# Routing steps of four links over half-batches a partition, and the light layer's first product behind them

## The chip, the cores and the metric

One core of a Trainium2 chip runs the whole kernel. The metric is the device time of one execution in microseconds; lower is better.

## What is computed

A decoder layer on x [2, 2048, 512]: self-attention with relative-position bias, cross-attention to 77 context tokens, and a feed-forward part with two layers, each block as x + f(layernorm(x)). The feed-forward part is what matters here: a light layer for every token, and a heavy one for the 512 tokens per batch that a coordinate descent of 50 steps picks.

```python
def ffn(x, gamma, w1, b1, w2, b2):
    h = rms_norm(x, gamma)
    h = jax.nn.gelu(h @ w1 + b1, approximate=False)
    return h @ w2 + b2
s = jnp.einsum('bnd,d->bn', x, routing_token)
constant = EPS * jnp.log(K_ROUTE)             # EPS 0.1, K_ROUTE 8
b0 = -jax.nn.relu(s)
def step(carry, _):                           # 50 times
    a_prev, b = carry
    a = constant - EPS * jax.nn.logsumexp((s + b) / EPS, axis=-1, keepdims=True)
    b = -jax.nn.relu(s + a)
    return ((a, b), None)
scores = jnp.exp((s + a + b) / EPS)
sel_scores, sel_idx = jax.lax.top_k(scores, 512)
light_out = ffn(x, light weights, hidden 256)       # all tokens
routed_out = ffn(x[sel_idx], heavy weights, hidden 2048)
```

## The kernel before

The program has three parts, each with its own order of instructions on every engine: `attention` (its last product of probs and v starts at 3013.6 us), `middle` (from 3072.4 us), which leaves the layer-normed tokens in DRAM, transposed and split in two terms (`scr["t3"]`), the tokens with what is to be added (`scr["xb"]`) and the routing values s (`scr["s"]`), and `routed` (from 3694.56 us), which the change touches. Nothing is scheduled by a tool: each engine (PE, ScalarE, VectorE, GpSimd, and SP, which issues the DMAs) has a list written out by hand, and semaphores tie the lists together.

In `routed` the values of both batches lie as `s_max` [128, 2, 16], token 128 t + p in partition p, with the maximum of a batch in a 17th column. A step (L1783 to L1797) takes on VectorE the minimum of s and the negated level (`low`) and the difference to its last column (`dif`), on ScalarE the Exp (L1713), on PE a product with a matrix of ones, which adds the 128 partitions and leaves 32 sums in every partition (L1609), on VectorE the sum of each batch's 16 (`total`, L1794), on ScalarE the Ln (L1715), on VectorE the new level (`neg_a`, L1797). PE then has work of its own between two steps: from the third step on, four matmuls of the light layer's first product (`hidden_of`, L1593), 192 in all, in eight chunks of 512 tokens with 24 matmuls each (two halves of the hidden size x 12 terms), so that they end with the last step. VectorE copies each finished half-chunk out of PSUM (`hidden_out`, L1772). ScalarE splits the light weights at step 0 (`wl1_hi`, L1719, which waits for the load of w1l), VectorE makes the rest of them at step 1 (`wl1_lo`, L1789), and from step 33 on ScalarE scales one of 16 pieces of the heavy layer's w1 behind each step (L1727).

SP loads the values, w1l and its gamma, chunks 0 and 1 of the tokens (`tokens_in`, L1522: two parts of 1 MB each into a buffer of two chunks), the light layer's w2, then chunk ch as soon as chunk ch - 2 has been multiplied, with four tiles of xb behind chunk 2 and the heavy layer's w1, the small constants and the rows b2 and places behind chunk 3.

Behind the steps come the scores (L1800 to L1807), 64 matmuls that spread them over the partitions (L1617), their copy (`rows`, L1731), the gelus of the light layer on ScalarE (L1736), five levels of a search for the 512th score (first L1830) with the light layer's second product between them, the choice and gather of the tokens, and the heavy layer (L1682 to L1704). VectorE waits for all weights ahead of `gain` (L1814), which comes before the first level.

## Time and profile before

| what | value |
|---|---|
| timed runs | 4121.46, 4125.23, 4127.27 us; median 4125.23 |
| profiled execution | 4132.32 us, its span 4130.5 us |
| granted TensorE clock, mean over the span | 0.974 |
| PE busy | 3930.1 us (95%), 18711 matmuls |
| VectorE / ScalarE / GpSimd busy | 58% / 49% / 65% |
| DMA | 350.50 MB, mean 85 GB/s |

All times inside the execution are counted from the start of the span. PE is busy nearly throughout, but this is an average over parts that differ; which engine or wait ends last in the stretch that is changed has to be read from that stretch. A matmul's busy time overlaps with that of the next, so the distance from start to start tells the rate.

### The profile page before, as it was taken

Reading aid. Unit: us, or ns where it says so; the run is one execution under the profiler, and the core shown is the slowest. Engines: PE = TensorE matmul, PEld = TensorE weight load, DVE = VectorE, ACT = ScalarE, POOL = GpSimd, SP = SyncE. Lnnn points to the kernel's source line nnn. Section 1 sums busy time; section 2 is a strip of 40 time slices with the busy share of each in tenths; the row PEclk is TensorE's granted clock in tenths of the full one; section 3 lists DMA queues with packets and bytes.
Section 4 is the critical chain, followed back from the end, with each engine's and each line's share of the span. In section 5 each row is a group of like instructions: output and inputs, shape, how many; then the busy total and the mean of one; then the engine's idle time right before and its main releaser. Section 6 shows DMA issues by size and latency. Waiting matters only on the chain. (4 is left out here: it accounts for less than half of the span.)

```text
span 4130.5 us, 59273 instructions
## 1 busy us (share of the span) xinstructions
PE 3930.1 (95%) x18711; PEld 2160.6 (52%) x18711; DVE 2411.3 (58%) x3315; ACT 2014.5 (49%) x3385; POOL 2693.8 (65%) x1406
## 2 busy tenths in 40 slices
PE   7979999999999999999999999999959999967899
PEld 6754444444444444444444444444338888854344
DVE  3346666666666666666666666666316777754400
ACT  2225555555555555555555555555424555533010
POOL 1008888888888888888888888888933444410010
PEclk9979999999999999999999999999979999979999
DMA  6632222232223342232222322232032333335610
GB/s 187 168 90 73 67 62 56 75 88 61 57 59 94 87 122 56 59 99 62 61 56 82 82 61 56 59 96 63 14 113 75 108 102 105 101 105 186 207 31 10
DMA packets 393921, 350.50 MB, mean 85 GB/s; under 512 B 193131, under 2 KB 267371, under 8 KB 392808
## 3 DMA queue, kind: packets, MB, share of 16 engines
q1 hardware_dynamic: 325864, 326.29, 27.2%
q10 hardware_dynamic: 66048, 16.78, 1.8%
q0 software_dynamic: 1920, 6.29, 0.5%
q8 instruction: 49, 0.80, 0.1%
q14 instruction: 40, 0.33, 0.0%
HBM read 142.89 MB, written 89.70 MB: 56 GB/s over the span
## 5 line engine op out<-in xcount | busy, mean ns | idle before, releaser
L254 POOL TENSOR_TENSOR acc<-acc,probs 128x1024 f32<-128x1024 f32 x896 | 2131.7, 2379 | 266.1 <-ACT probs L664 139.7
L771 DVE TENSOR_REDUCE maxes<-ps 128x1 f32<-128x1024 f32 x1024 | 1250.7, 1222 | 672.5 <-PE ps L482 667.9
L667 ACT ACTIVATE probs<-ps,far_bias 128x1024 f32<-128x1024 f32 (+7 forms) x1280 | 1022.1, 820 | 1017.4 <-DVE near_s L788 557.1
L517 PE MATMUL ps<-probs,v_head 128*64 128x512 f32 x4096 | 995.3, 607 | 5.3 <-ACT ctx_out L650 5.2
L482 PE MATMUL ps<-stacks 64*128 64x512 f32 x2048 | 752.3, 448 | 14.2 <-DVE maxes L771 11.1
L497 PE MATMUL ps<-stacks 64*128 64x512 f32 x1792 | 661.7, 449 | 0.0
L496 PE MATMUL ps<-stacks 128*128 128x512 f32 x2048 | 618.0, 418 | 0.0
L497 PEld LDWEIGHTS ps<-stacks 64*128 64x128 f32 x1792 | 276.7, 185 | 503.8 <-issue 343.4
L517 PEld LDWEIGHTS ps<-probs,v_head 128*64 128x64 f32 x4096 | 248.9, 136 | 487.7 <-issue 481.4
L496 PEld LDWEIGHTS ps<-stacks 128*128 128x128 f32 x2048 | 350.9, 188 | 215.8 <-issue 164.3
L788 DVE TENSOR_TENSOR near_s<-ps,near_bias 128x384 f32<-128x384 f32 (+2 forms) x576 | 284.7, 494 | 283.9 <-PE ps L497 261.0
L482 PEld LDWEIGHTS ps<-stacks 64*128 64x128 f32 x2048 | 306.6, 187 | 112.8 <-DVE maxes L771 60.8
L664 ACT ACTIVATE probs<-near_s 128x384 f32<-128x384 f32 (+2 forms) x576 | 271.5, 471 | 0.0
L465 PE MATMUL ps<-xn_hi,w_hi 128*128 128x512 f32 x512 | 207.8, 406 | 13.9 <-issue 5.1
L465 PE MATMUL ps<-xn_hi,w_lo 128*128 128x512 f32 x512 | 207.2, 405 | 0.0
L465 PE MATMUL ps<-xn_lo,w_hi 128*128 128x512 f32 x512 | 207.1, 404 | 0.0
L251 POOL TENSOR_TENSOR acc<-probs 128x1024 f32<-128x1024 f32 x64 | 152.8, 2388 | 44.2 <-issue 32.8
L440 PE MATMUL ps<-stacks,xn_hi 128*128 128x512 f32 x512 | 164.6, 403 | 11.4 <-DVE xn_lo L747 11.4
L1082 POOL TENSOR_TENSOR m_rs<-m_rs,m_expo 128x1 f32<-128x1 f32 x32 | 17.5, 548 | 240.2 <-DVE m_rs L1318 240.2
...
L223 POOL TENSOR_TENSOR rstd<-rstd,expo 128x1 f32<-128x1 f32 x32 | 18.0, 563 | 180.2 <-DVE rstd L734 180.2
...
## 6 DMA issues: line engine op xcount, KB each, us to landing
stacks<-c_k SPq DMA_DIRECT2D x128, 256.0 KB, 2.5
stacks<-c_q SPq DMA_DIRECT2D x128, 256.0 KB, 2.6
stacks<-c_d SPq DMA_DIRECT2D x256, 128.0 KB, 2.6
...
stacks<-c_q SPq DMA_DIRECT2D x128, 128.0 KB, 2.5
...
sums<-scr_inv SPq DMA_DIRECT2D x128, 128.0 KB, 2.9
scr_ctx<-ctx_out SPq DMA_DIRECT2D x128, 128.0 KB, 2.3
```

Source lines behind the costliest of these rows:

```text
L251: pool.tensor_tensor(acc[:, qb, :], probs[:, (st - 1) % PT_RING, :], pr, ALU.add).then_inc(s["summed"], 2)
L254: pool.tensor_tensor(acc[:, qb, :], acc[:, qb, :], pr, ALU.add).then_inc(s["summed"], 1)
L440: mm = pe.matmul(ps[:, 2 + v % 4, :], xs[i][:, k, t * P:(t + 1) * P], (wv_hi, wv_lo)[j][:, k, half * 512:(half + 1) * 512], start=at == 0, ...
L465: mm = pe.matmul(ps[:, proj_bank(m, tb), :], w[wi][:, kk, :], xs[xi][:, kk, tb * 512:(tb + 1) * 512], start=a == 0, stop=a == len(TERMS) - 1)
L482: mm = pe.matmul(ps[:, max_bank(n, qt, pair) + i, :], stacks[0:64, mside, QA, qt * P:(qt + 1) * P], stacks[0:64, mside, KX, kc * 512:(kc + ...
L496: return pe.matmul(out, stacks[:, side, KA, keys], stacks[:, side, QA, q], start=False, stop=True, skip_group_check=True)
L497: return pe.matmul(out, stacks[64:128, side, KX, keys], stacks[64:128, side, QB, q], start=False, stop=True, skip_group_check=True)
L517: mm = pe.matmul(ps[64 * half:64 * half + 64, PV, :], v_head[:, side, kt, :], probs[:, st % PT_RING, half * 512:(half + 1) * 512], start=k ...
L664: ins = act.activation(probs[:, st % PT_RING, a:z], near_s[:, st % 2, 0:z - a], ACT.Exp)
L667: ins = act.activation(probs[:, st % PT_RING, a:z], sc[:, a:z], ACT.Exp, bias=bias)
L771: dve.tensor_reduce(maxes[:, qt, pair:pair + 1], ps[:, bank:bank + 2, :], AX.XY, ALU.max).then_inc(s["max_done"], 1)
L788: dve.tensor_tensor(near_s[:, st % 2, 0:z - a], sc, near_bias[:, side, j0:j0 + z - a], ALU.add).then_inc(s["biased"], 1)
```

## The change

The values now lie as `s_half` [128, 2 x 16]: batch 0 in partitions 0 to 63, batch 1 in 64 to 127, 32 values in each. So a partition has one level. Everything is divided by EPS beforehand (`scaled`), and `lift` carries the level. A step is `arg` = min(ahead - log, 0) on VectorE, Exp on ScalarE with the sum of its 32 results into `sums`, a product of the block matrix `own` with that one column on PE, and Ln straight from PSUM on ScalarE. Beside them VectorE updates `lift` and makes the next `ahead`. Behind the last step the levels are spread again over all partitions by one more product with ones, and the scores are made in the old layout, for which `s_max` is loaded too.

`hidden_of` gives all 192 matmuls behind that product, none between steps. The 16 scalings of w1 move behind the gelus on ScalarE. SP issues chunk 0 ahead of w1l, and the heavy layer's weights behind the last chunk.

PE, from the start of `routed`; `r_t<-...` are the light layer's matmuls, `r_ex,r_ones` and `r_sums,r_own` those of a step. Before:

```order
L1580 MATMUL r_ps<-r_top_diag,r_ones 128x2
L1609 MATMUL r_ps<-r_ex,r_ones 128x32 x3
L1593 MATMUL r_ps<-r_t,r_wl_hi 128x512
L1593 MATMUL r_ps<-r_t,r_wl_lo 128x512
L1593 MATMUL r_ps<-r_t,r_wl_hi 128x512 x2
L1609 MATMUL r_ps<-r_ex,r_ones 128x32
L1593 MATMUL r_ps<-r_t,r_wl_lo 128x512
L1593 MATMUL r_ps<-r_t,r_wl_hi 128x512 x2
```

and now:

```order
L1588 MATMUL r_ps<-r_ones,r_top_wide 128x1
L1617 MATMUL r_ps<-r_sums,r_own 128x1 x50
L1622 MATMUL r_ps<-r_neg_a,r_ones 128x2
L1601 MATMUL r_ps<-r_t,r_wl_hi 128x512
L1601 MATMUL r_ps<-r_t,r_wl_lo 128x512
L1601 MATMUL r_ps<-r_t,r_wl_hi 128x512 x2
L1601 MATMUL r_ps<-r_t,r_wl_lo 128x512
```

What stood in pieces between the steps' products now follows them, behind the product with `neg_a`.

SP, from its first load in `routed`, before (`r_gelu<-in_w1l` is w1l, `r_gelu<-scr_xb` the xb tiles, `r_w<-in_w1h` the heavy w1):

```order
L1514 DMA r_s_max<-scr_s 128x4x4 x2
L1517 DMA r_gelu<-in_w1l 128x1024
L1517 DMA r_gamma_l<-in_gamma_l 128x4
L1522 DMA r_t<-scr_t 128x4x512 x4
L1532 DMA r_wl<-in_w2l 128x1024
L1532 DMA r_bl<-in_b1l 128x2
L1522 DMA r_t<-scr_t 128x4x512 x2
L1527 DMA r_gelu<-scr_xb 128x512 x4
L1522 DMA r_t<-scr_t 128x4x512 x2
```

and the end of the weights and what follows them, before:

```order
L1541 DMA r_above<-in_above 128x128
L1543 DMA r_b<-in_b2h 128x512
L1543 DMA r_places<-in_places 128x512
L1522 DMA r_t<-scr_t 128x4x512 x8
L1546 DMA out<-r_gelu 128x512
```

and now from the first load:

```order
L1518 DMA r_s_half<-scr_s 64x4x4 x4
L1524 DMA r_t<-scr_t 128x4x512 x2
L1536 DMA r_gelu<-in_w1l 128x1024
L1536 DMA r_gamma_l<-in_gamma_l 128x4
L1524 DMA r_t<-scr_t 128x4x512 x2
L1539 DMA r_s_max<-scr_s 128x4x4 x2
L1541 DMA r_wl<-in_w2l 128x1024
L1541 DMA r_bl<-in_b1l 128x2
L1524 DMA r_t<-scr_t 128x4x512 x2
L1529 DMA r_gelu<-scr_xb 128x512 x4
L1524 DMA r_t<-scr_t 128x4x512 x10
L1549 DMA r_w<-in_w1h 128x8192
```

Chunk 0 stands ahead of w1l now, and the last ten parts of chunks ahead of the heavy w1 instead of two of them.

VectorE, a stretch of the steps, before:

```order
L1783 TENSOR_TENSOR r_low<-r_s_max,r_neg_a 128x34
L1785 TENSOR_TENSOR r_dif<-r_low 128x32
L1772 COPY r_w<-r_ps 128x512
L1794 TENSOR_REDUCE r_total<-r_ps 128x2
L1797 SCALAR_TENSOR_TENSOR r_neg_a<-r_logs,r_low 128x2
L1783 TENSOR_TENSOR r_low<-r_s_max,r_neg_a 128x34
L1785 TENSOR_TENSOR r_dif<-r_low 128x32
```

and now, from the first step on (two `arg`, of steps 0 and 1):

```order
L1781 TENSOR_SCALAR r_ahead<-r_scaled,r_lift 128x32
L1801 TENSOR_SCALAR r_arg<-r_ahead,r_log 128x32 x2
L1803 TENSOR_TENSOR r_lift<-r_lift,r_log 128x1
L1805 TENSOR_SCALAR r_ahead<-r_scaled,r_lift 128x32
L1811 SCALAR_TENSOR_TENSOR r_wl_lo<-r_gelu,r_gamma_l,r_wl_hi 128x256 x4
L1801 TENSOR_SCALAR r_arg<-r_ahead,r_log 128x32
L1803 TENSOR_TENSOR r_lift<-r_lift,r_log 128x1
L1805 TENSOR_SCALAR r_ahead<-r_scaled,r_lift 128x32
```

The copy `r_w<-r_ps` (L1772) is gone from between the steps; all 16 stand behind the score.

The diff:

```diff
@@ -1397,12 +1397,11 @@
 NCHUNK = NB * S // TOKENS
 HIDDEN_TERMS = [(k, part, w) for k in range(KT) for part, w in ((0, 0), (0, 1), (1, 0))]
 HIDDEN = [(ch, m, at) for ch in range(NCHUNK) for m in range(LM) for at in range(len(HIDDEN_TERMS))]
-HIDDEN_FROM, HIDDEN_STEP = 2, 4
-HIDDEN_TO = HIDDEN_FROM + len(HIDDEN) // HIDDEN_STEP
+
+
 def hidden_of(i):
 
-    first = (i - HIDDEN_FROM) * HIDDEN_STEP
-    return HIDDEN[max(first, 0):max(first + HIDDEN_STEP, 0)]
+    return HIDDEN if i == N_ITERS else []
 
 
 def hidden_done(i):
@@ -1426,7 +1425,8 @@
 LIGHT_LAST = list(range(LIGHT_IN_STEP + 3 + len(LIGHT_AT_PLACE), NTILES))
 
 GAMMA_PIECES = HEAVY // 512
-GAMMA_FROM = 33
+
+HALF = P // NB
 
 
 def routed(nc, io, scr, out, index):
...
...
@@ -1502,6 +1505,7 @@
         out_rows = out.rearrange("b s d -> (b s) d")
         out_tiles = out_rows.rearrange("(j p) d -> j p d", p=P)
         scr_xb = scr["xb"].rearrange("(j p) d -> j p d", p=P)
+        scr_s = scr["s"].rearrange("(b q) p t -> b p q t", b=NB)
 
         def spread(ap):
 
@@ -1509,12 +1513,10 @@
 
         @block.sync
         def _(sp):
-            for b in range(NB):
-
-                sp.dma_start(s_max[:, b, 0:NT].rearrange("p (q t) -> p q t", t=TB),
-                             scr["s"].rearrange("(b q) p t -> b p q t", b=NB)[b]).then_inc(s["s_in"], 16)
-            for dst, name in LOADS_HIDDEN:
-                sp.dma_start(dst, io[name]).then_inc(s["wl1_in"], 16)
+            def s_in(b, half):
+
+                sp.dma_start(s_half[HALF * b:HALF * b + HALF, half, :].rearrange("p (q t) -> p q t", t=TB),
+                             scr_s[b, HALF * half:HALF * half + HALF]).then_inc(s["s_in"], 16)
 
             def tokens_in(ch):
 
@@ -1526,8 +1528,15 @@
 
                 sp.dma_start(xb[:, j % 4, :], scr_xb[j]).then_inc(s["xb_in"][j % 4], 16)
 
-            for ch in range(2):
-                tokens_in(ch)
+            for b in range(NB):
+                for half in range(2):
+                    s_in(b, half)
+            tokens_in(0)
+            for dst, name in LOADS_HIDDEN:
+                sp.dma_start(dst, io[name]).then_inc(s["wl1_in"], 16)
+            tokens_in(1)
+            for b in range(NB):
+                sp.dma_start(s_max[:, b, :].rearrange("p (q t) -> p q t", t=TB), scr_s[b]).then_inc(s["s_max_in"], 16)
             for dst, name in LOADS_LIGHT:
                 sp.dma_start(dst, io[name]).then_inc(s["light_in"], 16)
             for ch in range(2, NCHUNK):
@@ -1536,11 +1545,10 @@
                 if ch == 2:
                     for j in range(4):
                         xb_in(j)
-                if ch == 3:
-                    for dst, name in LOADS:
-                        sp.dma_start(dst[:], io[name]).then_inc(s["weights"], 16)
-                    for dst, name in ROWS:
-                        sp.dma_start(dst[:], io[name].partition_broadcast(P)).then_inc(s["weights"], 16)
+            for dst, name in LOADS:
+                sp.dma_start(dst[:], io[name]).then_inc(s["weights"], 16)
+            for dst, name in ROWS:
+                sp.dma_start(dst[:], io[name].partition_broadcast(P)).then_inc(s["weights"], 16)
             for j in range(NTILES):
                 sp.wait_ge(s["light"], j + 1)
                 sp.dma_start(out_tiles[j], light[:, j % 4, :]).then_inc(s["light_stored"][j % 4], 16)
@@ -1575,9 +1583,9 @@
         def _(pe):
             pe.wait_ge(s["const"], 1)
             pe.wait_ge(s["top_own"], 1)
-            pe.transpose(ps[0:NB, 0, 0:P], top[:], ident[:]).then_inc(s["top_turned"], 1)
-            pe.wait_ge(s["top_diag"], 1)
-            pe.matmul(ps[:, 1, 0:NB], ones[0:NB, :], top_diag[:], start=True, stop=True).then_inc(s["top_mm"], 1)
+            pe.transpose(ps[0:1, 0, 0:P], top[:], ident[:]).then_inc(s["top_turned"], 1)
+            pe.wait_ge(s["top_wide"], 1)
+            pe.matmul(ps[:, 1, 0:1], top_wide[:], ones[0:1, 0:1], start=True, stop=True).then_inc(s["top_mm"], 1)
 
             def hidden_mm(ch, m, at):
 
@@ -1606,10 +1614,14 @@
 
             for i in range(N_ITERS):
                 pe.wait_ge(s["ex"], i + 1)
-                pe.matmul(ps[:, 0, 0:NB * NT], ones[:], ex[:].rearrange("p b t -> p (b t)"), start=True, stop=True).then_inc(s["mm"], 1)
+                pe.matmul(ps[:, 0, 0:1], own[:], sums[:], start=True, stop=True).then_inc(s["mm"], 1)
                 for ch, m, at in hidden_of(i):
                     hidden_mm(ch, m, at)
 
+            pe.wait_ge(s["neg_a"], 1)
+            pe.matmul(ps[:, 0, 0:NB], ones[:], neg_a[:], start=True, stop=True).then_inc(s["neg_mm"], 1)
+            for ch, m, at in hidden_of(N_ITERS):
+                hidden_mm(ch, m, at)
             pe.wait_ge(s["score"], 1)
             for t in range(NT):
                 for b in range(NB):
@@ -1710,21 +1722,15 @@
             act.preload_act_table_set("natural_log_exp_and_others")
             for i in range(N_ITERS):
                 act.wait_ge(s["dif"], i + 1)
-                act.activation(ex[:], dif[:], ACT.Exp, scale=1.0 / ROUTE_EPS).then_inc(s["ex"], 1)
-                act.wait_ge(s["total"], i + 1)
-                act.activation(logs[:], total[:], ACT.Ln, scale=1.0 / K_ROUTE).then_inc(s["logs"], 1)
+                act.activation(powers[:], arg[:], ACT.Exp, accum_out=sums[:]).then_inc(s["ex"], 1)
+                act.wait_ge(s["mm"], i + 1)
+                act.wait_ge(s["lift"], i + 1)
+                act.activation(log[:], ps[:, 0, 0:1], ACT.Ln, scale=1.0 / K_ROUTE).then_inc(s["logs"], 1)
                 if i == 0:
                     act.wait_ge(s["wl1_in"], N_HIDDEN)
                     for k in range(KT):
                         ins = act.activation(wl1_hi[:, k, :], wl1[:, k, :], ACT.Identity, scale=gamma_l[:, k:k + 1])
                     ins.then_inc(s["wl1_hi"], 1)
-                piece = i - GAMMA_FROM
-                if 0 <= piece < KT * GAMMA_PIECES:
-                    if piece == 0:
-                        act.wait_ge(s["weights"], N_LOADS)
-                    k, n = divmod(piece, GAMMA_PIECES)
-                    part = w1[:, k, n * 512:(n + 1) * 512]
-                    act.activation(part, part, ACT.Identity, scale=gamma[:, k:k + 1]).then_inc(s["gam"], 1)
             act.wait_ge(s["arg"], 1)
             act.activation(ex[:], dif[:], ACT.Exp, scale=1.0 / ROUTE_EPS).then_inc(s["sc1"], 1)
             act.wait_ge(s["bc"], 1)
@@ -1735,6 +1741,10 @@
                 act.wait_ge(s["hidden"], q + 1)
                 act.activation(part, part, ACT.Gelu, bias=bl1[:, q % LM:q % LM + 1]).then_inc(s["gelu_l"], 1)
             act.wait_ge(s["weights"], N_LOADS)
+            for k in range(KT):
+                for n in range(GAMMA_PIECES):
+                    piece = w1[:, k, n * 512:(n + 1) * 512]
+                    act.activation(piece, piece, ACT.Identity, scale=gamma[:, k:k + 1]).then_inc(s["gam"], 1)
             for b in range(NB):
                 for t in range(HT):
                     act.wait_ge(s["tr"], HT * b + t + 1)
@@ -1755,16 +1765,20 @@
             for rows_of in shares:
                 for columns_of in shares:
                     dve.memset(own[rows_of, columns_of], 1.0 if rows_of == columns_of else 0.0)
-            dve.wait_ge(s["s_in"], 32)
-            dve.tensor_reduce(top[:], s_max[:, :, 0:NT], AX.X, ALU.max).then_inc(s["top_own"], 1)
+            dve.memset(log[:], 0.0)
+            dve.wait_ge(s["s_in"], 64)
+            dve.tensor_reduce(top[:], s_half[:], AX.XY, ALU.max).then_inc(s["top_own"], 1)
+            dve.tensor_scalar(scaled[:], s_half[:].rearrange("p h t -> p (h t)"), 1.0 / ROUTE_EPS, None, ALU.mult).then_inc(s["scaled"], 1)
             dve.wait_ge(s["top_turned"], 1)
-            dve.tensor_reduce(top_row[:], ps[0:NB, 0, 0:P], AX.X, ALU.max).then_inc(s["top_row"], 1)
-            dve.wait_ge(s["const"], 1)
+            dve.tensor_reduce(top_row[:], ps[0:1, 0, 0:P].rearrange("o (b p) -> o b p", b=NB), AX.X, ALU.max).then_inc(s["top_row"], 1)
             dve.wait_ge(s["top_row"], 1)
-            dve.tensor_scalar(top_diag[:], ident[0:NB, 0:NB], top_row[:], None, ALU.mult).then_inc(s["top_diag"], 1)
+            dve.tensor_scalar(top_wide[:].rearrange("o (b p) -> o b p", b=NB), top_row[:].unsqueeze(2).to_broadcast([1, NB, HALF]),
+                              1.0 / ROUTE_EPS, 0.0, ALU.mult, ALU.min).then_inc(s["top_wide"], 1)
             dve.wait_ge(s["top_mm"], 1)
-            dve.tensor_copy(s_max[:, :, NT], ps[:, 1, 0:NB]).then_inc(s["top"], 1)
-            dve.wait_ge(s["top"], 1)
+            dve.tensor_copy(lift[:], ps[:, 1, 0:1]).then_inc(s["lift"], 1)
+            dve.wait_ge(s["scaled"], 1)
+            dve.wait_ge(s["lift"], 1)
+            dve.tensor_scalar(ahead[:], scaled[:], lift[:], None, ALU.subtract).then_inc(s["ahead"], 1)
 
             def hidden_out(q):
 
@@ -1780,9 +1794,17 @@
                 dve.tensor_tensor(light[:, j % 4, :], ps[:, 4 + j % 4, :], xb[:, j % 4, :], ALU.add).then_inc(s["light"], 1)
 
             for i in range(N_ITERS):
-                dve.tensor_tensor(low[:], s_max[:], neg_a[:].unsqueeze(2).to_broadcast([P, NB, NT + 1]), ALU.min).then_inc(s["low"], 1)
-                dve.wait_ge(s["low"], i + 1)
-                dve.tensor_tensor(dif[:], low[:, :, 0:NT], spread(low[:, :, NT]), ALU.subtract).then_inc(s["dif"], 1)
+
+                dve.wait_ge(s["ahead"], i + 1)
+                if i:
+                    dve.wait_ge(s["logs"], i)
+                dve.tensor_scalar(arg[:], ahead[:], log[:], 0.0, ALU.subtract, ALU.min).then_inc(s["dif"], 1)
+                if i:
+                    dve.tensor_tensor(lift[:], lift[:], log[:], ALU.add).then_inc(s["lift"], 1)
+                    dve.wait_ge(s["lift"], i + 1)
+                    dve.tensor_scalar(ahead[:], scaled[:], lift[:], None, ALU.subtract).then_inc(s["ahead"], 1)
+                else:
+                    dve.sem_inc(s["ahead"], 1)
                 if i == 1:
                     dve.wait_ge(s["wl1_hi"], 1)
                     for k in range(KT):
@@ -1790,22 +1812,25 @@
                     ins.then_inc(s["wl1_lo"], 1)
                 for q in hidden_done(i - 1):
                     hidden_out(q)
-                dve.wait_ge(s["mm"], i + 1)
-                dve.tensor_reduce(total[:], ps[:, 0, 0:NB * NT].rearrange("p (b t) -> p b t", b=NB), AX.X, ALU.add).then_inc(s["total"], 1)
-
-                dve.wait_ge(s["logs"], i + 1)
-                dve.scalar_tensor_tensor(neg_a[:], logs[:], ROUTE_EPS, low[:, :, NT], ALU.mult, ALU.add).then_inc(s["neg_a"], 1)
-                dve.wait_ge(s["neg_a"], i + 1)
-
-            dve.tensor_tensor(low[:, :, 0:NT], s_max[:, :, 0:NT], spread(neg_a[:]), ALU.subtract).then_inc(s["kept"], 1)
+
+            dve.wait_ge(s["logs"], N_ITERS)
+            dve.tensor_tensor(lift[:], lift[:], log[:], ALU.add).then_inc(s["lift"], 1)
+            dve.wait_ge(s["lift"], N_ITERS + 1)
+            for b in range(NB):
+                first = slice(HALF * b, HALF * b + 1)
+                ins = dve.tensor_scalar(neg_a[first, b:b + 1], lift[first, :], ROUTE_EPS, None, ALU.mult)
+            ins.then_inc(s["neg_a"], 1)
+            dve.wait_ge(s["s_max_in"], 32)
+            dve.wait_ge(s["neg_mm"], 1)
+            dve.tensor_tensor(low[:], s_max[:], spread(ps[:, 0, 0:NB]), ALU.subtract).then_inc(s["kept"], 1)
             dve.wait_ge(s["kept"], 1)
-            dve.tensor_scalar(dif[:], low[:, :, 0:NT], 0.0, None, ALU.min).then_inc(s["arg"], 1)
+            dve.tensor_scalar(dif[:], low[:], 0.0, None, ALU.min).then_inc(s["arg"], 1)
             dve.wait_ge(s["arg"], 1)
             dve.tensor_scalar(kept[:], dif[:], LOWEST_EXP * ROUTE_EPS, None, ALU.is_ge).then_inc(s["kept"], 1)
             dve.wait_ge(s["kept"], 2)
             dve.wait_ge(s["sc1"], 1)
             dve.tensor_tensor(score[:], ex[:], kept[:], ALU.mult).then_inc(s["score"], 1)
-            for q in hidden_done(N_ITERS - 1):
+            for q in hidden_done(N_ITERS - 1) + hidden_done(N_ITERS):
                 hidden_out(q)
             dve.wait_ge(s["score"], 1)
             dve.tensor_scalar(weight[:], score[:], -1.0, 1.0, ALU.mult, ALU.add).then_inc(s["w"], 1)

```

## Rows read from the trace of the kernel before

**Rows 1.** The page: its first line.

```profile
span 4130.5 us, 59273 instructions
```

**Rows 2.** Timeline, end of the steps to the first level: start us, us, engine, line.

```profile
3803.53 0.19 DVE L1800 TENSOR_TENSOR r_low<-r_s_max,r_neg_a 128x32 f32<-128x32 f32 x1
...
3804.55 3.71 PE L1617 MATMUL r_ps<-r_ident,r_score 128*64 128x128 f32 x64 [0.71 <-DVE r_score L1807]
...
3808.32 1.87 ACT L1731 COPY r_rows<-r_ps 128x2048 f32<-128x2048 f32 x1 [4.12 <-PE r_ps L1617]
...
3810.31 2.35 DVE L1830 TENSOR_SCALAR_CACHE_REDUCE r_gelu<-r_rows,r_level 128x2048 f32<-128x2048 f32 x1 [4.16 <-ACT r_rows L1731]
...
3892.38 1.07 ACT L1741 COPY r_turned<-r_ps 128x512 f32<-128x512 f32 x2 [70.98 <-PE r_ps L1682]
```

**Rows 3.** The chain of waits in one step, in order of time: start us, us, what.

```profile
3723.36 0.20 DVE r_dif L1785
...
3723.59 0.24 ACT r_ex L1713
...
3723.87 0.42 PE r_ps L1609 x2
...
3724.54 0.21 ACT r_logs L1715
...
3725.43 0.24 ACT r_ex L1713
```

**Rows 4.** Timeline of the start.

```profile
3697.10 0.19 DVE L1759 TENSOR_REDUCE r_top<-r_s_max 128x2 f32<-128x32 f32 x1 [1.95 <-DMA r_s_max<-scr_s]
...
3699.32 0.20 DVE L1783 TENSOR_TENSOR r_low<-r_s_max,r_neg_a 128x34 f32<-128x34 f32 x1
...
3701.07 1.69 ACT L1719 ACTIVATE r_wl_hi<-r_gelu,r_gamma_l 128x256 fp32r<-128x256 f32 x4
...
3708.22 0.80 PE L1593 MATMUL r_ps<-r_t,r_wl_hi 128*128 128x512 f32 x1 [1.82 <-DMA r_t<-scr_t]
```

**Rows 5.** Windows (busy us by engine, PEclk, DMA share, GB/s), then PE's timeline.

```profile
3755.00:3757.00 2.00, 0.00 (x0) 0.00 (x0) 0.00 (x0) 0.13 (x1) 0.00 (x0) 0.55 1.01 356
...
3757.00:3759.00 2.00, 0.00 (x0) 0.00 (x0) 0.00 (x0) 0.00 (x0) 0.00 (x0) 0.50 1.05 398
...
3765.00:3767.00 2.00, 1.63 (x7) 1.11 (x6) 1.22 (x5) 0.20 (x1) 0.00 (x0) 0.89 0.00 0
...
3759.06 0.80 PE L1593 MATMUL r_ps<-r_t,r_wl_hi 128*128 128x512 f32 x1 [5.31 <-DMA r_t<-scr_t]
...
3759.65 0.63 PE L1593 MATMUL r_ps<-r_t,r_wl_lo 128*128 128x512 f32 x1
...
3760.07 1.06 PE L1593 MATMUL r_ps<-r_t,r_wl_hi 128*128 128x512 f32 x2
...
1004.60 0.40 PE L465 MATMUL ps<-xn_hi,w_hi 128*128 128x512 f32 x1
...
1004.84 0.40 PE L465 MATMUL ps<-xn_lo,w_hi 128*128 128x512 f32 x1
```

**Rows 6.** Timeline: the nearest operations to the new ones.

```profile
3507.27 0.63 ACT L1253 ACTIVATE m_junk<-m_xn 128x512 f32<-128x512 f32 x1 [0.17 <-ACT m_xn L1248]
...
3507.80 0.19 ACT L1253 ACTIVATION_READ_ACCUMULATOR m_junk<-m_xn 128x1 f32 x1
...
3812.91 0.38 PE L1622 MATMUL r_ps<-r_enough,r_own 128*128 128x1 f32 x2 [4.64 <-DVE r_enough L1833]
```

**Rows 7.** SP's timeline, and single issues with KB and us from issue to landing.

```profile
3730.85 1.50 SPq L1522 DMA_DIRECT2D r_t<-scr_t  x2
...
3736.52 0.43 SPq L1543 DMA_DIRECT2D r_places<-in_places  x1
...
r_t<-scr_t SPq DMA_DIRECT2D x1, 1024.0 KB, 8.2
...
r_places<-in_places SPq DMA_DIRECT2D x1, 256.0 KB, 17.1
```

More of the change, by code:

```diff
@@ L1450, in routed @@
         above = sb("above", [P, P])
-        s_max = sb("s_max", [P, NB, NT + 1])
-        top, top_row, top_diag = sb("top", [P, NB]), sb("top_row", [NB, 1]), sb("top_diag", [NB, NB])
-        low = sb("low", [P, NB, NT + 1])
+        s_max = sb("s_max", [P, NB, NT])
+        s_half = sb("s_half", [P, 2, NT])
+        scaled, ahead, arg, powers = (sb(n, [P, 2 * NT]) for n in ("scaled", "ahead", "arg", "powers"))
+        sums, log, lift = (sb(n, [P, 1]) for n in ("sums", "log", "lift"))
+        top, top_row, top_wide = sb("top", [P, 1]), sb("top_row", [1, NB]), sb("top_wide", [1, P])
+        low = sb("low", [P, NB, NT])
         dif, ex = sb("dif", [P, NB, NT]), sb("ex", [P, NB, NT])
-        total, logs = sb("total", [P, NB]), sb("logs", [P, NB])
         neg_a = sb("neg_a", [P, NB])
@@ L1486, in routed @@
         HOT, TURN = 0, 6
-        s = {n: sem(n) for n in """weights const zero s_in top_own top_turned top_row top_diag top_mm top gam low dif ex mm total logs neg_a arg kept sc1 sc score w
+        s = {n: sem(n) for n in """weights const zero s_in s_max_in top_own top_turned top_row top_wide top_mm lift scaled ahead gam dif ex mm logs neg_a neg_mm arg kept sc1 sc score w
             bc bcr t1 cnt en en_mm f1 f2 base over mm1 r1 r2 r3s sel mm2 p1 p2 place hot hot_mm pairs pairs_tr parts4 gain edge_own edge_mm edge picked index
```

## Prediction

> **What bounds the kernel now.** I read the page first for the span, then the chain of waits that ended last, then the timeline around the routing steps, and the transfers by issue. Attention and the middle part (to 3690 us) are untouched; from the first level search on (L1830, 3810.31 [rows 2]) the program is again the same. So only the stretch from 3697 to 3810 us changes. The profiled execution took 4132.3 us around a span of 4130.5 [rows 1]; the median of the timed runs is 4125.2, 7.1 lower. I work out a difference inside the profile and add it to the median.
>
> In that stretch the chain goes through the steps themselves: Exp, product, Ln, again and again [rows 3]. A step is low, dif, Exp, product with ones, row sum, Ln, neg_a: seven links, 1.84 us from one Exp to the next (3723.59, 3725.43 [rows 3]). The light layer's first product runs in the gaps, for nothing. The first step starts at 3699.32 [rows 4], the last is over at 3803.53 [rows 2]: 104.2 us, of which 50 x 1.84 = 92.0 are the steps; the rest is a start at the lower clock, the preparation of wl1 and one wait of 5.31 us for a chunk of tokens [rows 5]. Nearly all of the 192 matmuls is hidden, and with them the six chunks (12.6 MB) that are loaded meanwhile.
>
> **The change, part by part.**
>
> *Start.* Four loads of the scores instead of two come first on SP, at about half a microsecond an issue, so the last lands about 0.95 later. From the first reduction to the first step are 2.22 us today (3697.10 to 3699.32 [rows 4]); `ahead` adds 0.22. First `arg`: 3697.10 + 0.95 + 2.22 + 0.22 = 3700.5.
>
> *A step.* Four links. arg to Exp: 0.23, as dif to Exp (3723.36 to 3723.59 [rows 3]). Exp to PE: 0.28 (to 3723.87 [rows 3]), and the accumulator read behind it: after a 0.63 us ACTIVATE the read ends at 0.53 + 0.19 = 0.72 [rows 6], so 0.09 more. A one-column product: 0.38 at the lower clock [rows 6] and 0.04 to its reader. Ln: 0.21 [rows 3] and 0.03. Sum 1.26; Ln now reads PSUM and waits for two semaphores, for which I add 0.01: 1.27. Below: 1.05, if PE were at the full clock (half of 0.38 less) and the Ln read cost nothing. Above: 1.45, with 0.1 each for the PSUM read and the second wait. I take 1.27, since all four links have a near row. 50 x 1.27 = 63.5. `lift` and the next `ahead` (two DVE operations, 0.4) lie beside Exp and product. Gone from between the steps are the 16 scalings of w1, whose places ScalarE now fills behind the gelus, ahead of a wait of 71 us that it has today [rows 2]: nothing.
>
> The Trainium skill (ScalarE: Activation LUTs, Rules for kernel authors) budgets about 0.3 us per ACTIVATE plus 0.83 ns an element; by that Exp and Ln would cost 0.2 us more a step, 10 us in all. The trace has 0.24 and 0.21 for them, and the sum goes by the trace.
>
> *wl1.* SP now issues chunk 0 (2.1 MB) ahead of w1l. Today w1l goes first and ScalarE scales it at 3701.07, while chunk 0 behind it lands at 3708.22 [rows 4]. The same 2.6 MB must now be there before w1l is: about 3708.2 again. ScalarE waits for it behind the Ln of step 0 (over near 3701.7), scales for 1.69 us, and Exp of step 1 goes at 3710 instead of 3702; DVE's wl1_lo, about as long, holds one later `arg` 0.6. Stall 8.5; at best 5 (a clean pair of parts lands in 8.8 [rows 7]), at worst 13, if chunk 1 is served beside it.
>
> *End of the steps.* 3700.5 + 63.5 + 8.5 = 3772.5; then lift, two neg_a and the product that spreads them, 0.9: the light product starts at T = 3773.4. The score (five small operations) is made beside its first matmuls; PE reads it only behind the run.
>
> *The run.* At the full clock such a matmul follows its like in 0.233 us, at the lower in 0.42 to 0.43 [rows 5]: 24 of a chunk take 5.6, all 192 44.7. But the token buffer holds two chunks, and during the steps nothing is loaded beyond them. Chunk c+2 is asked for when chunk c is done, and lands 8.8 later (the second part issued 0.6 behind the first, 8.2 to landing [rows 7]). Behind the wait that began at 3753.75 (3759.06 - 5.31) the clock averages 0.55 from 3755 to 3757, so it fell within 1.5 us; PE resumed at 3759.06 and had the full clock back only after 3765, some 6.3 us later [rows 5]. A chunk after a wait so costs 6.0 for 14 matmuls and 2.3 for ten: 8.3. From T: chunk 0 to 8.3 (PE did little in the steps), chunk 1 to 13.9; chunk 2, asked for at 8.3, lands 17.1, done 25.4; chunk 3, behind 1 MB of xb, landed 25.1, done 31.0; chunk 4 asked 25.4, lands 34.2, done 42.5; chunk 5 done 48.1; chunk 6 lands 51.3, done 59.6; chunk 7 done 65.2. Three waits of 3.2 us. No row has one of 3.2; the nearest are 5.31 and 4.64 [rows 5, 6], and as the fall came within 1.5 I take 65.2. With the clock up after the waits the same reckoning gives 59.5.
>
> The Trainium skill (TensorE: Matmul & The Clock Gate, Loop structure matters more than you think) wants matmuls back to back and warns of a DMA wait between them, which lowers the clock. Read for the word "run", it promises 44.7 us here; read for the waits, 65.2.
>
> *Behind the run.* Spreading the scores (3.74, to ScalarE's start at 3808.32) and copying the rows (1.87) [rows 2] now follow it: 3773.4 + 65.2 + 5.8 = 3844.4. The weights are the second gate: SP issues them behind chunk 7, at T + 48.1 = 3821.5, when chunk 6 is still in the queue. Today chunk 3 and the weights together take from 3730.85 to 3753.6 (places: issued 3736.52, 17.1 to landing), 22.8 us [rows 7]: 3844.3. DVE waits for them ahead of `gain`, with eight short operations, 1.1 us, up to the first level: 3845.4, against 3810.3. **Sum: +35.1 us.** Behind it the order is as today. 4125.2 + 35.1 = 4160.3 us.
>
> **The rivals.**
>
> *Everything cheap.* Step 1.10, wl1's stall 5.5, no restart at the lower clock: T = 3761.9, weights asked for at T + 45.1, first level 3830.9: +20.6, 4145.8. Each is an end of a bound; against it, three must meet.
>
> *The run stays at the lower clock.* A chunk then takes 10.3 and hides its successor's load: 82.6 us, first level 3861.8: +51.5, 4176.7. For it: waits every 17 us. Against: in [rows 5] PE was back at the full clock 6.3 us after it resumed. A step of 1.45 alone gives +9: 4169.3.
>
> *Not slower: the run is fed.* If w1l is as early as today, a step costs 1.10 and the queue keeps PE's pace, the row copy ends at 3700.5 + 55.0 + 0.9 + 44.7 + 5.8 = 3806.9 against 3810.2 [rows 2]: 3.3 less, 4121.9. With that start (3756.4) it decides at a run of 48 us; with mine even 44.7 is 13.7 too long. Against it: chunks, xb and weights are 18.4 MB, at the 0.36 to 0.40 MB a microsecond of a full queue [rows 5] 46 to 51 us by themselves, and the first is asked for only behind chunk 0.
>
> *The change does not do what it says.* The order shows 50 products with nothing between and 192 matmuls behind them; left out.
>
> **How the numbers follow.** The forecast with its own spread (4152 to 4168): 0.66. Everything cheap: 0.14. Dear step, or run at the lower clock: 0.15. Fed run: 0.05, of which 0.02 beyond the 0.2% (8 us) that a measurement of this kernel can tell from no change. The range leaves out the tails: 4146 to 4171. Faster 0.02, same 0.03, slower 0.95.
>
> **What would show it.** A step of 1.2 to 1.35 us with PE at 1.2 GHz; a gap of 5 to 13 us before the second Exp, ended by w1l; the first matmul of the run near 3773, the last 58 to 66 us later, with three or more idle times of 2 to 5 us ended by chunk loads and half clock behind them; weights landing within 3 us of the row copy's end; the first level near 3845; 16 scalings that nobody waits for. Wrong would be a run near 45 us, or a first level before 3818.

## The result: 1.3% slower, and 22 us slower than forecast

The changed kernel takes 4181.9 us (median of four, 4172.6 to 4186.2) against 4125.6 for the kernel before beside it: ratio 1.013 (95% interval 1.011 to 1.0151), +56.3 us. The forecast was 4160.3 us with a range of 4146 to 4171. The direction was right, the time outside the range. Of two kernels further down (e1, e6) one of four executions took more than twice as long (11026 and 9417 us), and their medians here are those of the other three.

The profiled execution took 4185.0 us:

```profile
span 4183.2 us, 59385 instructions
```

That is 52.7 more than the span of [rows 1]. Where it lies is read from three marks:

| mark | before | after | difference |
|---|---|---|---|
| this part begins (first GpSimd instruction) | 3694.56 | 3696.34 | +1.8 |
| first level search | 3810.31 | 3862.48 | +52.2 |
| start to first level | 115.75 | 166.14 | +50.4 |
| first level to end of span | 320.2 | 320.7 | +0.5 |

The parts ahead of this one are the same in all kernels here, but their end wanders between 3682 and 3696 from one profiled execution to another, for a reason that no run shows. So the experiments are compared by the stretch **from the start of this part to the first level**, and medians beside it. Each such stretch is read from one profiled execution. Forecast for it: 3845.4 - 3694.56 = 150.8. It missed by 15.3 us.

The start, in the timeline of the changed kernel (start us, us, engine, line; in brackets the idle time before and what ended it):

```profile
3700.55 0.18 DVE L1770 TENSOR_REDUCE r_top<-r_s_half 128x1 f32<-128x32 f32 x1 [3.52 <-DMA r_s_half<-scr_s]
...
3703.04 0.24 DVE L1801 TENSOR_SCALAR r_arg<-r_ahead,r_log 128x32 f32<-128x32 f32 x1
...
3711.44 1.70 ACT L1732 ACTIVATE r_wl_hi<-r_gelu,r_gamma_l 128x256 fp32r<-128x256 f32 x4 [6.95 <-DMA r_gamma_l<-in_gamma_l]
3713.05 0.21 ACT L1725 ACTIVATE r_powers<-r_arg 128x32 f32<-128x32 f32 x1
```

The first `arg` starts 6.70 us into the part, where 3700.5 - 3694.56 = 5.94 was forecast. At a regular step the second Exp would have started at 3704.60 + 0.27; it started at 3713.05: 8.2 late, because ScalarE waited for the light weights behind chunk 0. The load that ended the wait was not w1l, issued at 3700.38 and there 8.6 us later (3709.0), but the 2 KB of gamma_l issued after it (3701.14, there 10.3 us later, 3711.4). This answers to [rows 4].

One step of the changed kernel, which answers to [rows 3], in the same view:

```profile
3716.31 0.24 DVE L1801 TENSOR_SCALAR r_arg<-r_ahead,r_log 128x32 f32<-128x32 f32 x1 [0.97 <-ACT r_log L1728]
...
3716.59 0.23 ACT L1725 ACTIVATE r_powers<-r_arg 128x32 f32<-128x32 f32 x1 [0.38 <-DVE r_arg L1801]
...
3716.72 0.19 ACT L1725 ACTIVATION_READ_ACCUMULATOR r_powers<-r_arg 128x1 f32 x1
...
3716.96 0.58 PE L1617 MATMUL r_ps<-r_sums,r_own 128*128 128x1 f32 x2 [0.96 <-ACT r_powers L1725]
3717.58 0.17 ACT L1728 ACTIVATE r_log<-r_ps 128x1 f32<-128x1 f32 x1 [0.68 <-PE r_ps L1617]
3717.86 0.24 DVE L1801 TENSOR_SCALAR r_arg<-r_ahead,r_log 128x32 f32<-128x32 f32 x1 [0.97 <-ACT r_log L1728]
```

0.28 + 0.37 + 0.62 + 0.28 = 1.55 us, where 1.27 was forecast. The product alone has 0.62 to its reader instead of 0.42. Of the 47 distances between the third `arg` and the last, 45 are 1.55 or 1.56.

The windows (busy us of PE, PEld, DVE, ACT, POOL, then PEclk, DMA share, GB/s) show the steps, and then the first wait in the run:

```profile
3740.00:3790.00 50.00, 18.78 (x64) 16.06 (x64) 17.57 (x97) 15.78 (x96) 0.00 (x0) 0.50 0.00 0
...
3806.00:3808.00 2.00, 0.00 (x0) 0.00 (x0) 0.00 (x0) 0.00 (x0) 0.00 (x0) 1.00 1.05 362
3808.00:3810.00 2.00, 1.91 (x5) 1.52 (x6) 0.00 (x0) 0.00 (x0) 0.00 (x0) 0.55 1.05 364
3810.00:3812.00 2.00, 2.00 (x7) 1.56 (x6) 0.00 (x0) 0.00 (x0) 0.00 (x0) 0.59 1.05 399
3812.00:3814.00 2.00, 2.00 (x11) 1.62 (x10) 0.69 (x1) 0.00 (x0) 0.00 (x0) 1.00 1.02 380
```

In the steps the clock stands at 0.50, the lower level (1.2 GHz), PE is busy for 38% of the time, and the DMA engines move nothing. The run that follows, in PE's timeline, its first matmul and its waits:

```profile
3790.81 0.77 PE L1601 MATMUL r_ps<-r_t,r_wl_hi 128*128 128x512 f32 x1
...
3808.09 0.71 PE L1601 MATMUL r_ps<-r_t,r_wl_hi 128*128 128x512 f32 x1 [4.30 <-DMA r_t<-scr_t]
...
3816.11 0.50 PE L1601 MATMUL r_ps<-r_t,r_wl_hi 128*128 128x512 f32 x1 [0.65 <-DMA r_t<-scr_t]
...
3824.51 0.50 PE L1601 MATMUL r_ps<-r_t,r_wl_hi 128*128 128x512 f32 x1 [2.63 <-DMA r_t<-scr_t]
...
3840.92 0.50 PE L1601 MATMUL r_ps<-r_t,r_wl_hi 128*128 128x512 f32 x1 [3.54 <-DMA r_t<-scr_t]
...
3850.02 0.50 PE L1601 MATMUL r_ps<-r_t,r_wl_hi 128*128 128x512 f32 x1 [1.73 <-DMA r_t<-scr_t]
```

It goes from T = 3790.81 to 3855.8 (the last matmul, 0.40, starts at 3855.39), 65.0 us, 12.85 of them waiting. Not every wait cost the clock: behind those of 4.30, 2.63 and 3.54 us the windows have some 4 us at the lower level, behind those of 0.65 and 1.73 us they show 1.00 (3816 to 3818, 3850 to 3854). Its end and the weights, which answer to [rows 2], in the timeline of all engines:

```profile
3838.67 0.62 SPq L1549 DMA_DIRECT2D r_w<-in_w1h x1
...
3843.30 0.81 SPq L1551 DMA_DIRECT2D r_places<-in_places x1
...
3855.72 3.71 PE L1629 MATMUL r_ps<-r_ident,r_score 128*64 128x128 f32 x64
...
3859.48 1.86 ACT L1737 COPY r_rows<-r_ps 128x2048 f32<-128x2048 f32 x1 [67.76 <-PE r_ps L1629]
...
3861.52 0.19 DVE L1839 TENSOR_TENSOR r_gain<-r_score,r_weight 128x32 f32<-128x32 f32 x1 [4.91 <-DMA r_places<-in_places]
...
3862.48 2.35 DVE L1855 TENSOR_SCALAR_CACHE_REDUCE r_gelu<-r_rows,r_level 128x2048 f32<-128x2048 f32 x1
...
3945.02 1.07 ACT L1751 COPY r_turned<-r_ps 128x512 f32<-128x512 f32 x2 [62.65 <-PE r_ps L1694]
```

The copy of the rows ends at 3861.3, the places land at 3861.5 and hold the gain: both gates within 0.2 us, as forecast. The scalings of w1 have gone into ScalarE's long wait, which shrank from 71 to 62.7 us and costs nothing.

### The profile page after: what moved, and what is told of

It is laid out like the page before. It is cut to its first block and busy times, and to the rows that moved or that the text cites. A ratio compares the mean times of both kernels' runs of the same rounds, so it can differ in the third digit from the quotient of the medians.

```text
span 4183.2 us, 59385 instructions
## 1 busy us (share of the span) xinstructions
PE 3941.1 (94%) x18713; PEld 2178.5 (52%) x18713; DVE 2402.9 (57%) x3269; ACT 2017.8 (48%) x3435; POOL 2693.7 (64%) x1406
## 5 line engine op out<-in xcount | busy, mean ns | idle before, releaser
L440 PE MATMUL ps<-stacks,xn_hi 128*128 128x512 f32 x512 | 163.9, 402 | 11.3 <-DVE xn_lo L747 11.3
L1205 PEld LDWEIGHTS m_ps<-m_turned,m_wq 128*128 128x128 f32 x1024 | 122.6, 196 | 4.5 <-ACT m_turned L1278 2.0
```

The costliest lines, as they stand in the source:

```text
L440: mm = pe.matmul(ps[:, 2 + v % 4, :], xs[i][:, k, t * P:(t + 1) * P], (wv_hi, wv_lo)[j][:, k, half * 512:(half + 1) * 512], start=at == 0, ...
```

## The experiments

Two questions. Is the missing 15 us the price of a step at the lower clock? And what makes up the 65 us of the run? Eight kernels ran, e1 to e4 beside the kernel before with a median of 4126.6, e5 to e8 with one of 4125.4. "Links" are the operations of one step in their order, with the time of a step in us.

| kernel | steps | light product | start to first level | median us |
|---|---|---|---|---|
| before | 7 links, 1.84 | in the steps | 115.8 | 4125.6 |
| e4_old_run_behind | 7 links, 2.07 | behind | 179.7 | 4186.1 (one run) |
| the change | 4 links, 1.55 | behind | 166.1 | 4181.9 |
| e1_w1l_first | 4 links, 1.55 | behind | 158.8 | 4172.5 |
| e2_filled_gaps | 4 links, 1.34 | behind | 152.2 | 4170.8 (one run) |
| e5_run_ring4 | 4 links, 1.55 | behind | 145.2 | 4151.7 |
| e6_weights_in_steps | 4 links, 1.55 | behind | 163.3 | 4172.9 |
| e3_steps_mixed | 4 links, 1.35 | in the steps | 99.0 | 4108.6 |
| e7_mixed_w1l_first | 4 links, 1.35 | in the steps | 91.6 | 4101.0 |
| e8_mixed_ring4 | 4 links, 1.35 | in the steps | 89.2 | 4099.5 |

### e2_filled_gaps: the steps at the full clock

```diff
+                if i == 2:
+                    pe.wait_ge(s["t3_in"][0], 32)
+                    pe.wait_ge(s["wl1_lo"], 1)
+                if i >= 2:
+                    for k in range(3):
+                        pe.matmul(ps[:, 7, :], wl1_hi[:, k, 0:P], t3[:, 0, 0, k, :], start=True, stop=True)
```

Three matmuls behind each step's product, whose result nobody reads.

> The changed kernel with three matmuls of 128x512 behind each step's product from the third step on, whose results nobody reads. Theory (the one-column product takes 0.60 us because PE does so little in the steps that it stays at 1.2 GHz): the granted clock in the steps goes to 1.00 within some 10 us, the product to 0.38, the step from 1.55 to 1.33 to 1.38, and chunk 0 of the run starts at the full clock (5.6 instead of 7.4 us); first matmul of the run near 3781 instead of 3790.8, whole about 4170. Rival (0.60 is the price of this shape, or of loading own each time, whatever the clock): clock 1.00 but product still 0.6, step 1.55 or more.

Its windows, and one step in its timeline:

```profile
3740.00:3780.00 40.00, 35.15 (x150) 21.00 (x149) 16.06 (x89) 14.49 (x88) 0.00 (x0) 1.00 0.00 1
```

```profile
3740.43 0.24 DVE L1807 TENSOR_SCALAR r_arg<-r_ahead,r_log 128x32 f32<-128x32 f32 x1 [0.77 <-ACT r_log L1734]
...
3741.08 0.38 PE L1617 MATMUL r_ps<-r_sums,r_own 128*128 128x1 f32 x2
...
3741.50 0.17 ACT L1734 ACTIVATE r_log<-r_ps 128x1 f32<-128x1 f32 x1 [0.47 <-PE r_ps L1617]
3741.77 0.24 DVE L1807 TENSOR_SCALAR r_arg<-r_ahead,r_log 128x32 f32<-128x32 f32 x1 [0.76 <-ACT r_log L1734]
```

Clock 1.00, the product 0.38 instead of 0.58, the distance to Ln 0.42 instead of 0.62, a step 1.34 instead of 1.55; the stretch is 14.0 us shorter than in the change. More work on PE made this part faster: the product sits in a chain, and its price goes with a clock that idle gaps let fall. Up to T the stretch is 9.9 shorter, 8.6 of it between the third `arg` and the last, the 0.2 a step; the run, which now began at the full clock and waited 11.3 in all, took 60.6 instead of 65.0 (3780.53 to 3841.16).

### e1_w1l_first: w1l ahead of the tokens

```diff
-            tokens_in(0)
             for dst, name in LOADS_HIDDEN:
                 sp.dma_start(dst, io[name]).then_inc(s["wl1_in"], 16)
+            tokens_in(0)
             tokens_in(1)
```

> The changed kernel with one edit: SP issues w1l and its gamma ahead of chunk 0 again. Theory (ScalarE's wait for w1l holds the second step, and nothing hides it): the gap in front of the second Exp goes from 8.2 us to about 1.7, the first matmul of the run moves from 3790.8 to about 3784, and the whole from 4181.9 to about 4175. Rival (the wait only moves: what was held up at the start comes back in the run, because the chunks land later): the same time within 2 us.

```profile
3698.85 1.69 ACT L1732 ACTIVATE r_wl_hi<-r_gelu,r_gamma_l 128x256 fp32r<-128x256 f32 x4
...
3700.44 0.22 ACT L1725 ACTIVATE r_powers<-r_arg 128x32 f32<-128x32 f32 x1
```

ScalarE scales right behind the first Ln, and the second Exp comes 2.65 us behind the first (3697.79) instead of 9.74. The stretch falls by 7.3, all of it ahead of the run, and the median by 9 (ratio to before 1.0113, 1.0093 to 1.0133): the order of the light weights and chunk 0 cost seven of the 50 us, and the rival, by which the wait would only move into the run, did not hold.

### e5_run_ring4: four chunks there when the run begins

```diff
+        with nc.sbuf_tensor("r_more", [P, 2, 2, KT, TOKENS], F32R) as more:
+            pass
...
+        chunks = [t3[:, 0], t3[:, 1], more[:, 0], more[:, 1]]
...
-            for ch in range(2, NCHUNK):
-                sp.wait_ge(s["hidden_mm"], LM * (ch - 1))
+            tokens_in(2)
+            tokens_in(3)
+            for j in range(4):
+                xb_in(j)
+            for ch in range(RING, NCHUNK):
+                sp.wait_ge(s["hidden_mm"], LM * (ch - RING + 1))
                 tokens_in(ch)
```

`more` takes the memory of `r3` and `y`, which are used only later.

> The changed kernel with one thing altered: the tokens of the light layer's first product lie in a ring of four chunks instead of two (the two more lie where the heavy gathers come later), so that four chunks are there when the run begins, and chunk 4 is asked when chunk 0 is done. In the changed kernel TensorE waited 12.8 us for chunks in a run of 64.9 us, and after each wait it had some 4 us at the lower clock. Theory (the run's waits for transfers, and the clock lost behind them, are what the run costs over 192 products at the full clock, some 46 us): no wait for a chunk is left, the lower clock is seen once, at the run's start, the run takes 46 to 49 us, the weights are asked at some 24 us into it and are there before the row copy ends, and the time falls by 16 to 19 us, to some 4163 to 4166. Rival (the transfers are bound by the DMA engines' rate, and a deeper ring only moves the waits to the last chunks, where the weights share the queues): TensorE still waits 8 us or more, the run takes 57 us or more, and the time falls by less than 8 us. Second rival (the clock falls in a run without waits too): the run takes over 60 us with no wait in it. The step stays at 1.55 us with every theory.

A window in its run, the last matmul of the run and the gates behind it:

```profile
3806.00:3810.00 4.00, 4.00 (x19) 3.29 (x18) 1.28 (x2) 0.00 (x0) 0.00 (x0) 1.00 1.10 426
```

```profile
3822.66 0.39 PE L1607 MATMUL r_ps<-r_more,r_wl_hi 128*128 128x512 f32 x1
...
3824.48 0.19 DVE L1845 TENSOR_TENSOR r_gain<-r_score,r_weight 128x32 f32<-128x32 f32 x1 [0.61 <-DMA r_places<-in_places]
...
3828.74 2.35 DVE L1861 TENSOR_SCALAR_CACHE_REDUCE r_gelu<-r_rows,r_level 128x2048 f32<-128x2048 f32 x1 [3.34 <-ACT r_rows L1743]
```

No wait for a chunk; the clock is back within some 4 us of the run's start and stays; the run goes from 3777.2 to 3823.05, 45.8 us. The stretch falls by 21.0: 19.2 from the run, 1.0 from the gate, since the level now begins right behind the row copy, and 0.9 ahead of the run, most of it in ScalarE's wait for gamma_l. That wait scatters: it took between 5.66 and 6.95 us in the five kernels that issue it in the same order (the change, e2, e3, e5, e6), so differences of about 1 us between stretches prove nothing. Neither rival held: the DMA engines keep up (426 GB/s beside the run), and the clock does not fall in a run without waits. More was gained than expected: the run came out just under the 46 to 49 us of the theory, and the median is 30 us under that of the change instead of 16 to 19. Of these 30 the stretch has 21; in the profiled executions this part also began 12.8 us earlier (3683.59), which is not the ring's.

### e6_weights_in_steps: the heavy weights asked early

The eight loads of `LOADS` and `ROWS` moved ahead of the loop over chunks, so that they run while the DMA engines idle.

> The changed kernel with the heavy weights (4.9 MB with their rows) asked right behind the light layer's own, while the routing steps still run and the DMA engines idle, instead of behind the last chunk. Theory (in the changed kernel the weights share the queues with the last chunk, which landed 12.6 us after it was asked instead of some 8, and the places land with them just behind the row copy): chunk 7 lands in time or with a wait of under 1 us (it was 1.7), the gain no longer waits for places, the first level starts as the row copy ends, and from the start of this part to the first level it is 162 to 165 us where the changed kernel had 166.1; the time falls by 1 to 4 us. Rival (the gate of the first level is the row copy alone, and the last chunk's wait is the chunk's own): within 1 us of the changed kernel.

```profile
3856.87 2.35 DVE L1855 TENSOR_SCALAR_CACHE_REDUCE r_gelu<-r_rows,r_level 128x2048 f32<-128x2048 f32 x1 [3.91 <-ACT r_rows L1737]
```

The level waits for the row copy alone and chunk 7 for nothing; the stretch is 2.8 us shorter, as expected. But not all of this belongs to the weights. 1.3 us lie ahead of the run, in the wait for gamma_l, where nothing was changed. And chunk 7 comes without a wait in e1 and e4 too, where the weights are still late: their runs take 64.2 us, that of e6 64.4. What is left is 1.0 us between the end of the run and the first level. The median, 4172.9, is 9 lower than that of the change, and the two ranges overlap (4164.7 to 4178.9, 4172.6 to 4186.2). So the late weights, which the prediction gave a section of their own, were worth about 1 us and at most 3.

### e3_steps_mixed and e4_old_run_behind: the two halves apart

e3 has the change's steps with four matmuls of the light layer in each; e4 has the steps of before with the whole product behind them (weights and scalings where the change has them, w1l first).

```diff
 def hidden_of(i):
-    return HIDDEN if i == N_ITERS else []
+    first = (i - HIDDEN_FROM) * HIDDEN_STEP
+    return HIDDEN[max(first, 0):max(first + HIDDEN_STEP, 0)]
```

> The changed kernel, but the light layer's product again four matmuls a step from the third on; all else of the change stays. Theory (the loss is the separate run, 65 us that were hidden before, and the four-link step is itself a gain): step 1.35 to 1.45 us at the full clock, steps and light product over near 3790, no run; the weights, still issued last, land near 3791; first level near 3792 and the whole about 4108, faster than before by about 17. Rival (four matmuls of 0.233 do not fit in the shorter gap, and the step becomes as long as the old one): step 1.84, first level 3806 to 3812, whole 4125.

> The kernel before with the other half of the change alone: old seven-link steps, all 192 matmuls behind the last step, weights behind the last chunk, scalings of w1 behind the gelus; w1l still first. Theory: the steps run at 1.2 GHz, 2.07 us each, last product near 3805; the run takes 65 us as in the changed kernel and the first level starts about 72 us after its first matmul, near 3876; whole about 4191, 10 slower than the changed kernel. Rival (the run is only this slow because the new layout's loads are in its way): run below 60 us, whole below 4185.

A step of e3, and its first level:

```profile
3730.92 0.23 DVE L1803 TENSOR_SCALAR r_arg<-r_ahead,r_log 128x32 f32<-128x32 f32 x1
...
3732.25 0.24 DVE L1803 TENSOR_SCALAR r_arg<-r_ahead,r_log 128x32 f32<-128x32 f32 x1 [0.76 <-ACT r_log L1730]
...
3782.57 2.35 DVE L1857 TENSOR_SCALAR_CACHE_REDUCE r_gelu<-r_rows,r_level 128x2048 f32<-128x2048 f32 x1 [0.83 <-ACT r_rows L1739]
```

And one of e4, from one Exp to the next:

```profile
3741.32 0.23 ACT L1708 ACTIVATE r_ex<-r_dif 128x32 f32<-128x32 f32 x1 [0.68 <-DVE r_dif L1777]
...
3741.61 0.64 PE L1605 MATMUL r_ps<-r_ex,r_ones 128*128 128x32 f32 x2 [1.43 <-ACT r_ex L1708]
...
3743.39 0.23 ACT L1708 ACTIVATE r_ex<-r_dif 128x32 f32<-128x32 f32 x1 [0.68 <-DVE r_dif L1777]
```

The new steps alone take 16.7 us off the stretch (115.75 to 99.04), and e3 is faster than the kernel before by 0.4%: 4108.6 us, ratio 0.9959 (0.9945 to 0.9974). Moving the product, with the weights and scalings that follow it, adds 63.9 (115.8 to 179.7); e4's run takes 64.2 us with the old layout, so the rival, by which the new layout's loads make the run slow, did not hold. Behind the steps, with w1l first in both, the new ones are worth 20.9 (e4 to e1). The change joins a gain of some 20 to a loss of some 64, and hangs 7 us of its load order on top. A step of before takes 2.07 us at the lower clock (0.50 from 3740 to 3790) instead of 1.84, so taking the filler out of the gaps makes either kind of step dearer by about 0.2.

### e7_mixed_w1l_first and e8_mixed_ring4: better than both

e7 is e3 with the edit of e1; e8 adds the ring of e5, with the heavy weights behind the request of chunk 5.

> The mixed version of before (the change's four-link steps with four products of the light layer in each, 4108.6 us, 99.0 us from the start of this part to the first level), with the light layer's first weights asked ahead of the tokens as well. In the mixed version ScalarE waited 5.9 us for gamma_l behind its first Ln. Theory (that wait lies on the chain of steps as it did in the changed kernel, where the same edit took off 7.3 us): the start to the first level takes 91 to 93 us, and the time is 4101 to 4103 us. Rival (in the mixed version the steps later catch on the chunks of tokens, which are asked at fixed products, and an earlier start of the steps only lengthens TensorE's waits for chunks, 4.9 us there): 96 us or more, and 4105 us or more.

> The mixed version with both: the light layer's first weights asked first, a ring of four chunks, and the heavy weights behind the request of chunk 5, some 20 us into the steps. Theory (what is left on the path is the chain of 50 steps with TensorE at the full clock, 1.35 to 1.40 us each, and the stages around it): no wait for a chunk, none for places, 82 to 87 us from the start to the first level, and 4092 to 4097 us, the best of all. Rival (with four products in the gap of each step TensorE is itself the bound, at some 1.45 us a step): 88 to 92 us, and 4098 to 4102. Second rival (the weights that load beside the steps hold back chunks 6 and 7): a wait of 3 us or more for one of them.

The first level of e7, then two waits of PE and the first level of e8:

```profile
3773.93 2.35 DVE L1857 TENSOR_SCALAR_CACHE_REDUCE r_gelu<-r_rows,r_level 128x2048 f32<-128x2048 f32 x1 [1.20 <-ACT r_rows L1739]
```

```profile
3699.53 0.80 PE L1610 MATMUL r_ps<-r_t,r_wl_hi 128*128 128x512 f32 x1 [2.39 <-DMA r_t<-scr_t]
...
3750.61 0.50 PE L1610 MATMUL r_ps<-r_more,r_wl_hi 128*128 128x512 f32 x1 [0.87 <-DMA r_more<-scr_t]
...
3773.83 2.35 DVE L1864 TENSOR_SCALAR_CACHE_REDUCE r_gelu<-r_rows,r_level 128x2048 f32<-128x2048 f32 x1 [4.16 <-ACT r_rows L1746]
```

e7 came out as its theory had it: 91.6, from a start at 3682.30, and 4101.0 us (0.9947, 0.9931 to 0.9964); with w1l first the new steps so take 24.1 us off the stretch of before. e8 took 89.2, from 3684.63, and 4099.5 us (0.9944, 0.9923 to 0.9965): above the 82 to 87 expected. The number fits its first rival, the reason doesn't: its regular steps are 1.33 to 1.38 us, no slower for their four matmuls. What is missing are two waits for chunks: the first (3699.53) on chunk 0 put the fifth `arg` 4.69 us behind the fourth instead of 1.54, the second, of 0.87, put 2.50 us instead of 1.35 behind the fortieth; without them it would be some 85, as expected. Between e7 and e8 the medians (1.6 us apart) don't decide; in the stretch the ring and the earlier weights together are worth 2.4 us where the steps already space the loads.

## Why the prediction missed, point by point

- **A step: the term that failed.** The prediction has "A one-column product: 0.38 at the lower clock [rows 6]". That row was at the full clock. The windows of the kernel before around it say so:

```profile
3810.00:3812.00 2.00, 0.00 (x0) 0.00 (x0) 1.69 (x1) 1.97 (x3) 0.00 (x0) 1.00 0.00 0
3812.00:3814.00 2.00, 1.09 (x3) 0.66 (x4) 1.39 (x7) 2.00 (x5) 0.00 (x0) 0.81 0.00 0
```

  PE had idled for 4.64 us before that product and the prediction took idle for slow, but the clock had not fallen yet: in windows of half a microsecond it is 1.00 up to 3813.0, 0.73 to 3813.5 and 0.50 behind that, and the product ran from 3812.91 to 3813.29. A product at the lower clock stood in the same timeline at the start of this part, where the window shows 0.50:

```profile
3698.51 0.58 PE L1580 MATMUL r_ps<-r_top_diag,r_ones 2*128 2x2 f32 x2 [0.70 <-DVE r_top_diag L1764]
```

```profile
3698.00:3700.00 2.00, 0.58 (x2) 0.49 (x2) 0.89 (x5) 0.23 (x1) 0.00 (x0) 0.50 0.67 190
```

  With 0.58 and 0.04 for 0.42 the step comes to 1.47. The other 0.08 are hand-overs: arg to Exp 0.28 for 0.23, and Ln to arg 0.28 for 0.24, though Ln itself took 0.17 for 0.21. Over 50 steps 10 us are the clock and 4 the hand-overs: 14 of the 15.3 us (two steps with 0.35 more in the trace make it 14.7). e2 confirms it from the other side: at the full clock the product has the forecast 0.42, and the step of 1.34 still holds the 0.08 of the hand-overs, so these are not the clock's; why they are longer no run shows. The lower bound of 1.05 was wrong too: it halved the 0.38 once more for the full clock, where 0.38 is the price; at the full clock e2's step is 1.34. The upper bound of 1.45 failed because it widened the links of ScalarE and never the product, and so the range did.
- **The page on ScalarE.** The sum by its budget of about 0.3 us per ACTIVATE (the Trainium skill, ScalarE: Activation LUTs, Rules for kernel authors) would have been 10 us longer and so nearer to the result, but not for its reason: Exp took 0.23 and Ln 0.17, both below that budget.
- **Start:** four issues took 2.67 us and the values were there 0.7 later than forecast: +0.8.
- **wl1:** 8.5 forecast; 8.2 for the second Exp, and 0.4 for the third (3715.03, 1.98 behind it): right in size. The load that ended the wait was gamma_l's, 2.4 us behind w1l, which the prediction does not name; counted from the start of the part it came 1.5 us later than forecast, and the Ln ahead of the wait 1.0 later, which nearly cancels.
- **The run:** 65.2 forecast, 65.0 measured, but by two errors that cancel. Waits: three of 3.2 (9.6) forecast, five of 12.85 in all. Clock: at 0.229 a matmul (e5) 192 take 44.0, so 65.0 - 12.85 - 44.0 leaves 8.2, where 10.9 was forecast. Both have four stretches at the lower clock, the run's start and three waits, but PE was back at the full clock some 4 us after it resumed, not 6. That the total came out within 0.2 is luck. The Trainium skill (TensorE: Matmul & The Clock Gate, Loop structure matters more than you think) warns of DMA waits between matmuls because PE then runs cold, and the change agrees for its three longer waits: half clock behind each. Without waits e5 took 45.8, 1.1 over the 44.7 worked out for such a run.
- **Where the 15.3 lie:** the run began 94.5 us into the part instead of 78.8, so 15.6 late: 14.7 from the steps, 0.8 from the start. All that follows came out within 0.3. Added to the forecast, 15.3 us give 4175.6, which is outside the range without the rest.
- **Behind the run:** T + 72.0 forecast for the first level, T + 71.7 measured; weights asked at T + 48.1, measured T + 47.9.
- **Rivals.** "Everything cheap" rested on a step of 1.10, less than any step here. "The run stays at the lower clock" gives 4176.7, near the result, and did not happen: the window from 3812 shows 1.00. "Not slower: the run is fed" named a run of 48 us as the point from which it decides. e5 reached 45.8, and was still slower than before, 4151.7 us (ratio 1.0071, 1.0054 to 1.0088): with T so late a fed run is not enough, as the prediction said of its own T.
- **Unforeseen:** the remaining 5.9 us between medians and stretch (56.3 - 50.4): 1.8 ahead of this part and 0.5 behind it in the profiles, the other 3.6 between the profiled executions and the medians. No run explains them.
